# Token blocks of a gated linear attention and MoE layer: another order of the four engines' work, own buffers for the router's rows, a one-pass gate product

## The chip, the cores and the metric

One Trainium2 chip, one core. The metric is device time in microseconds (us) of one execution. A core has five engines with queues of their own: PE (TensorE, matmuls; PEld is its weight load), DVE (VectorE), ACT (ScalarE), POOL (GpSimd) and SP (SyncE, here the issuer of most DMAs). They meet only at semaphores. Everything is fp32; products that matter for precision are made of three f32r ("fp32r") products of a high and a low part.

## What is computed

```python
x = x + attn(layernorm(x))        # x: 2 x 8192 x 512, 16 heads of 32, chunks of 64
x = x + ffn(layernorm(x))
# attn
q, k, v = x@Wq+bq, x@Wk+bk, x@Wv+bv
alpha = 0.9 * sigmoid(silu(x@Wg1+bg1) @ Wg2 + bg2) + 0.1      # Wg1: 512 x 16
intra = softmax(causal(q k^T / sqrt(32))) v                   # within a chunk of 64
inter_t = q_t S ;  S = alpha_t * S + k_t v_t^T                # a state over all tokens
# ffn: 64 experts, top 8, 256 places each, hidden 384
routed = sum over the token's experts of w_e * down_e(silu(gate_e x) * up_e x)
shared = (silu(x @ gate) * (x @ up)) @ down
```

## The kernel before

`phase_tokens` goes over the 16384 tokens in 64 blocks of 256; `phase_experts` then goes over the 64 experts and is not touched. The change lies in `phase_tokens`.

For each block the kernel makes: the norm (`norm1`, `rstd1`, `shift1`, `normalise`), its transpose XT as high and low part (`xt`, `xt_evac`, `xt_low`), the gate (`gate1`: 512 to 16, `silu1`, `gate2`: 16 to 512, tanh and `alpha`), q, k, v (`project`, `values`), the running product of alpha within half chunks (`decays`), its inverse (`products`, `inverse`: two reciprocals on DVE), and with both the decayed q and k on POOL (`unpair`, `fold`, `decayed_k`, `decayed_q`). The inter part needs k turned back to tokens (`ktok`), four outer products (`state_updates`) and the state's steps (`state`). The attention proper has four units u = 0 to 3, each 128 tokens by 8 heads. A unit is a chain: `scores` (PE), `softmax_a` (mask, maximum, decayed scores; DVE), `exp` (eight exponentials with sums; ACT), `softmax_b` (divide; DVE), `turn_probs` (PE), `weights` (DVE), `outputs` (PE), `ot` (eviction; ACT). Then: `turn_out`, `residual` with the variance, `rstd2` (POOL), `norm2`, the transpose `x2t`, the router (`router`, `lt`, `turn_logits`, `route_a` to `route_c`, counts in `positions`), and the shared feed forward (`gate_up` 0 to 2, `gu`, `hidden`, `hidden_high`, `hidden_low`, `down`, `total`).

The order on each engine is written out by hand, one list per engine, in a loop over pairs of blocks (PE's body: 16 blocks). PE's step (L1057) is `feed(t)`, all of the feed forward of block t, and then `attend(t+1)`, all four units of block t+1 mixed with the projections of block t+2. The last `attend` projects a block 64 that doesn't exist. An engine stops at a wait, and all that is behind it in its queue stops too.

What ties the lists together beside the data are the buffers. PE writes every product other than scores, probabilities and outputs into four PSUM banks; `BANK_OF` says which job has which bank, and `take` (L709) waits until the bank's last job has been read. The router's transposed rows go into XT, the same buffer as those of the attention, so `x2t` on ACT (L603) waits until block t+1's values are made, and `xt_evac` (L545) until `gate_up` is done. KD, QD, PV, RI and AL exist once. POOL's order in the loop is `unpair`, `fold`, `decayed_k`, `rstd2(0)`, `decayed_q`, `rstd2(1)`, `rstd1` (L525 to L531). `gate2` (L756) is an f32 product; L762 is its matmul. The helper L729 to L731 (`split_product`) records all three-part products.

## Time and profile before

| | us |
|---|---|
| median of 3 runs (lowest, highest) | 4608.77 (4606.5, 4610.91) |
| the profiled execution's own time | 4610.58 |
| its span on the core | 4608.7 |
| granted TensorE clock, mean over the span | 0.992 |
| PE busy | 4433.4 (96%) |
| DVE busy | 3520.7 (76%) |
| ACT busy | 2271.6 (49%) |
| POOL busy | 1333.8 (29%) |

The span runs from the first instruction to the last. Busy time is the time in which at least one of an engine's instructions runs; a busy PE is not PE at its peak, because matmuls are pipelined and overlap in the record. So the length of a piece of PE's work is read here as its pitch, from its start to the start of the next piece. The token phase runs to about 3680, the expert phase from there to the end.

### The profile page before, as it was taken

Reading aid. Unit: us, or ns where it says so; the run is one execution under the profiler, and the core shown is the slowest. Engines: PE = TensorE matmul, PEld = TensorE weight load, DVE = VectorE, ACT = ScalarE, POOL = GpSimd, SP = SyncE. Lnnn points to the kernel's source line nnn. Section 1 sums busy time; section 2 is a strip of 40 time slices with the busy share of each in tenths; the row PEclk is TensorE's granted clock in tenths of the full one; section 3 lists DMA queues with packets and bytes.
Section 4 is the critical chain, followed back from the end, with each engine's and each line's share of the span. In section 5 each row is a group of like instructions: output and inputs, shape, how many; then the busy total and the mean of one; then the engine's idle time right before and its main releaser. Section 6 shows DMA issues by size and latency. Waiting matters only on the chain. (4 is left out here: it accounts for less than half of the span.)

```text
span 4608.7 us, 182901 instructions
## 1 busy us (share of the span) xinstructions
PE 4433.4 (96%) x74416; PEld 3859.5 (84%) x74416; DVE 3520.7 (76%) x7639; ACT 2271.6 (49%) x7475; POOL 1333.8 (29%) x1275
## 2 busy tenths in 40 slices
PE   6999999999999999999999999999999969999998
PEld 5888888888888888888888888888888769999998
DVE  5777777777777777777777777777777778888887
ACT  4444444444444444444444444444444446666665
POOL 2111111111111111222221111111111156666666
PEclk9999999999999999999999999999999989999999
DMA  2001001011010001000001000001010079999997
GB/s 67 32 31 31 31 31 36 32 35 33 31 31 32 32 31 32 32 31 31 32 32 35 31 31 32 31 31 36 32 36 32 32 242 266 270 265 270 267 267 194
DMA packets 195037, 358.24 MB, mean 78 GB/s; under 512 B 16736, under 2 KB 92896, under 8 KB 194352
## 3 DMA queue, kind: packets, MB, share of 16 engines
q1 hardware_dynamic: 160848, 269.47, 17.6%
q0 software_dynamic: 33632, 79.73, 7.8%
q8 instruction: 547, 8.96, 0.8%
q14 instruction: 10, 0.08, 0.0%
HBM read 243.87 MB, written 107.50 MB: 76 GB/s over the span
## 5 line engine op out<-in xcount | busy, mean ns | idle before, releaser
L591 ACT ACTIVATE PR<-PR,MX 128x64 f32<-128x64 f32 x2048 | 682.7, 335 | 736.6 <-DVE MX L1186 736.6
L477 POOL TENSOR_TENSOR RI<-PV,AL 128x512 f32<-128x512 f32 x65 | 78.7, 1212 | 2448.5 <-DVE PV L1140 2448.5
L729 PE MATMUL bank<-XTh,wsguh 128*128 128x256 f32 x1536 | 447.1, 291 | 0.1
L1678 PE MATMUL ebank<-XH,WH 128*128 128x256 f32 x1536 | 431.3, 281 | 7.3 <-DVE XL L1760 7.3
L730 PE MATMUL bank<-XTl,wsguh 128*128 128x256 f32 x1536 | 430.4, 280 | 0.0
L731 PE MATMUL bank<-XTh,wsgul 128*128 128x256 f32 x1536 | 430.4, 280 | 0.0
L1678 PE MATMUL ebank<-XH,WL 128*128 128x256 f32 x1536 | 429.8, 280 | 0.0
L1678 PE MATMUL ebank<-XL,WH 128*128 128x256 f32 x1536 | 429.6, 280 | 0.0
L1753 DVE TENSOR_TENSOR WL<-WS,WH 128x768 fp32r<-128x768 f32 (+1 forms) x455 | 370.8, 840 | 16.2
L591 ACT ACTIVATION_READ_ACCUMULATOR PR<-PR,MX 128x1 f32 x2048 | 383.0, 187 | 0.0
L1615 ACT ACTIVATE WH<-WS 128x768 fp32r<-128x768 f32 (+1 forms) x455 | 325.2, 747 | 26.6 <-DMA WS<-in_L_ffn_w_down_dram 26.6
L729 PE MATMUL bank<-XTh,wkh 128*128 128x256 f32 x1040 | 315.4, 303 | 0.0
L729 PE MATMUL bank<-XTh,wqh 128*128 128x256 f32 x1040 | 305.1, 293 | 0.0
L1678 PEld LDWEIGHTS ebank<-XH,WH 128*128 128x128 f32 x1536 | 289.4, 188 | 10.1 <-issue 7.7
L730 PE MATMUL bank<-XTl,wqh 128*128 128x256 f32 x1040 | 292.6, 281 | 0.0
L731 PE MATMUL bank<-XTh,wql 128*128 128x256 f32 x1040 | 292.5, 281 | 0.0
L730 PE MATMUL bank<-XTl,wkh 128*128 128x256 f32 x1040 | 291.4, 280 | 0.0
L731 PE MATMUL bank<-XTh,wkl 128*128 128x256 f32 x1040 | 291.2, 280 | 0.0
L1678 PEld LDWEIGHTS ebank<-XL,WH 128*128 128x128 f32 x1536 | 288.3, 188 | 2.5
L729 PEld LDWEIGHTS bank<-XTh,wsguh 128*128 128x128 f32 x1536 | 289.6, 189 | 0.6 <-issue 0.6
L730 PEld LDWEIGHTS bank<-XTl,wsguh 128*128 128x128 f32 x1536 | 290.0, 189 | 0.0
L1678 PEld LDWEIGHTS ebank<-XH,WL 128*128 128x128 f32 x1536 | 289.8, 189 | 0.0
(228 smaller groups left out, 13243.6 us busy)
## 6 DMA issues: line engine op xcount, KB each, us to landing
WS<-in_L_ffn_w_gate_dram SPq DMA_DIRECT2D x65, 768.0 KB
WS<-in_L_ffn_w_up_dram SPq DMA_DIRECT2D x65, 768.0 KB
WS<-in_L_ffn_w_down_dram SPq DMA_DIRECT2D x65, 768.0 KB
norm_rows<-XR SPq DMA_DIRECT2D x64, 576.0 KB, 3.5
X<-in_L_attn_x_dram SPq DMA_DIRECT2D x66, 512.0 KB, 3.7
out_dram<-X SPq DMA_DIRECT2D x64, 512.0 KB, 2.9
CR<-token_counts,count_at POOLq DMA_INDIRECT x136
XG<-norm_rows,row_at POOLq DMA_INDIRECT x132, 6.2
```

What stands on the lines that cost most here:

```text
L477: nc.gpsimd.tensor_tensor(inverse[:, :, 0:half], PV[:, :, :], running[:, :, HC:half:-1], ALU.mult).then_inc(folded.sem, 1)
L591: ins = nc.scalar.activation(PR[b][:, j, :], PR[b][:, j, :], ACT.Exp, bias=MX[b][:, j:j + 1], scale=1.0, accum_out=SU[b][:, j:j + 1])
L729: nc.tensor.matmul(out, sh, mh, start=first, stop=False)
L730: nc.tensor.matmul(out, sh, ml, start=False, stop=False)
L731: return nc.tensor.matmul(out, sl, mh, start=False, stop=last)
L1615: nc.scalar.activation(WH[t.buf][:, cols], WS[t.buf][:, cols], ACT.Copy).then_inc(wh_ready.sem, 1)
L1678: last = nc.tensor.matmul(bank[HID[m]][:, a * CAP:(a + 1) * CAP], w, x[odd][:, c, :], start=(c == 0 and i == 0), stop=(c == KC - 1 and i = ...
L1753: v.tensor_tensor(WL[t.buf][:, cols], WS[t.buf][:, cols], WH[t.buf][:, cols].bitcast(f32), ALU.subtract).then_inc(wl_ready.sem, 1)
```

## The change

In words:

- The router's transposed rows get buffers of their own, XB; `x2t` now waits for the last block's `gate_up` only, and `xt_evac` for the last projections. KD is now RI and s1 is t1, in place.
- `gate2` is one f32r product. `s1` and Wg2 lie in partitions 0, 32 and 64 as high, low and high part (`COPIES`), so that one product of 128 rows sums all three terms. `s1_high` (ACT) and `s1_low` (DVE, 32 partitions) are new; Wg1, Wg2 and bg1 are loaded three times in the setup, and Wg2 is split there.
- Unit 0 of block n = t+1 is moved into block t's feed part on all engines; `ktok` and the first half of `state` too. Units 1 to 3 stay beside the projections of block m = t+2.
- ACT: `normalise(p)`, p = t+3, ahead of `gu(n, 0)` and of the exponentials of unit 0. DVE: both reciprocals behind `weights(n, 3)`; `softmax_a` is split in two, `residual` and `route_b` too; `route_c` (the counts) is ahead of `route_rows`. POOL: `rstd2(0)` first, `rstd1` last.
- PE's jobs have other banks, and a job's wait is worked out from `JOBS` (bank, block ahead).
- The first and the last steps are written out; block 64 and SP's two last loads of X are gone.

```diff
+JOBS = {
+    "GU0": (2, 0), "RLT": (1, 0), "KTok0": (3, 1), "GU1": (0, 0), "KTok1": (1, 1), "GU2": (3, 0), "DN0": (2, 0), "DK": (0, 1),
+    "DN1": (1, 0), "G1": (3, 2), "Qa": (1, 2), "G2a": (2, 2), "G2b": (3, 2), "Ka": (1, 2), "ATr0": (3, 1), "Qb": (0, 2),
+    "Kb": (2, 2), "V0": (1, 2), "ATr1": (3, 1), "X2Ta": (2, 1), "X2Tb": (3, 1), "V1": (0, 2), "RL": (1, 1)}
+ORDER = list(JOBS)
+
...
+        XB = [sb(f"XB{i}", [P, KC, TB], f32r) for i in "hl"]
...
-        KD = sb("KD", [P, KC, TB])
+        KD = RI
...
             def unpair(t):
 
                 pool.wait_ge(inverted.sem, t.value(inverted))
-                pool.wait_ge(kd_ready.sem, t.value(kd_ready, back=1))
+                pool.wait_ge(scored.sem, t.value(scored, back=1))
+                pool.wait_ge(ktok_filled.sem, t.value(ktok_filled, back=1))
                 apart(pool, pool_apart)
...
+            def step(t):
+                n = t.next()
+                m = t.next(2)
+                p = t.next(3)
+                rstd2(n, 0)
+                unpair(m)
+                rstd2(n, 1)
+                fold(m)
+                decayed_k(m)
+                decayed_q(m)
+                rstd1(p)
 
             rstd1(Turn(0, 0))
...
+            def xt_evac(t, k):
+
+                act.wait_ge(v_filled.sem, t.value(v_filled, back=1))
+                act.wait_ge(q_filled.sem, t.value(q_filled, back=1))
+                act.wait_ge(k_filled.sem, t.value(k_filled, back=1))
+                act.wait_ge(xt_filled.sem, t.value(xt_filled, k))
+                nc.scalar.activation(XT[0][:, 2 * k:2 * k + 2, :], XT_BANK[k].rearrange("p (a b) -> p a b", a=2),
+                                     ACT.Copy).then_inc(xh_ready.sem, 1)
 
             def gate1(t):
                 act.wait_ge(g1_filled.sem, t.value(g1_filled))
                 act.wait_ge(s1_ready.sem, t.value(s1_ready, back=1))
                 nc.scalar.activation(t1[:, :], bank_of("G1")[0:GP, 0:TB], ACT.Tanh, bias=b1h[:, :], scale=0.5).then_inc(g1_tanh.sem, 1)
                 nc.scalar.activation(z1[:, :], bank_of("G1")[0:GP, 0:TB], ACT.Identity, bias=b1[:, :], scale=1.0).then_inc(g1_tanh.sem, 1)
+
+            def s1_high(t):
+                act.wait_ge(s1_made.sem, t.value(s1_made))
+                act.wait_ge(g2_filled.sem, t.value(g2_filled, back=1))
+                nc.scalar.activation(sg[:, :], s1[:, :], ACT.Copy).then_inc(s1h_ready.sem, 1)
...
+            def x2t(t, k):
+                act.wait_ge(gu_filled.sem, t.value(gu_filled, back=1))
+                act.wait_ge(x2t_filled.sem, t.value(x2t_filled, k))
+                nc.scalar.activation(XB[0][:, 2 * k:2 * k + 2, :], bank_of("X2Ta" if k == 0 else "X2Tb")[:, :]
+                                     .rearrange("p (a b) -> p a b", a=2), ACT.Copy).then_inc(x2h_ready.sem, 1)
...
+            def step(t):
+                n = t.next()
+                m = t.next(2)
+                p = t.next(3)
+                gate1(m)
+                exp(n, 1)
+                s1_high(m)
+                ot(n, 0)
+                q_evac(m, 0)
+                gate2(m, 0)
+                gate2(m, 1)
+                alpha(m)
+                exp(n, 2)
+                ot(n, 1)
+                k_evac(m, 0)
+                exp(n, 3)
+                ot(n, 2)
+                q_evac(m, 1)
+                k_evac(m, 1)
+                ot(n, 3)
+                x2t(n, 0)
+                x2t(n, 1)
+                lt(n)
+                normalise(p)
+                gu(n, 0)
+                hidden_high(n, 0)
+                exp(m, 0)
+                ktok_evac(m, 0)
+                gu(n, 1)
+                hidden_high(n, 1)
+                ktok_evac(m, 1)
+                router_exp(n)
+                gu(n, 2)
+                xt_evac(p, 0)
+                xt_evac(p, 1)
+                hidden_high(n, 2)
...
+            def take(job, t):
+
+                for name, at in jobs_back(job):
+                    if t.next(at).exists:
+                        ev, k = READ[name]
+                        pe.wait_ge(ev.sem, t.next(at).value(ev, k))
+                        break
                 return bank_of(job)
...
+                if k == 0:
+                    pe.wait_ge(a_masked.sem, t.next(-1).value(a_masked, 0))
...
+            def s1_low(t):
+                dve.wait_ge(s1h_ready.sem, t.value(s1h_ready))
+                v.tensor_tensor(sg[32:64, :], s1[32:64, :], sg[32:64, :].bitcast(f32), ALU.subtract).then_inc(s1_ready.sem, 1)
...
+            def step(t):
+                n = t.next()
+                m = t.next(2)
+                p = t.next(3)
+                scores_part(n, 1)
+                decay_part(n, 1)
+                silu1(m)
+                state(n, (2, 3))
+                s1_low(m)
+                softmax_b(n, 1)
+                weights(n, 1)
+                scores_part(n, 2)
+                decay_part(n, 2)
+                decays(m)
+                softmax_b(n, 2)
+                products(m)
+                weights(n, 2)
+                scores_part(n, 3)
+                decay_part(n, 3)
+                residual(n, 0)
+                variance2(n, 0)
+                softmax_b(n, 3)
+                weights(n, 3)
+                inverse(m, 0)
+                inverse(m, 1)
+                norm2(n, 0)
+                residual(n, 1)
+                variance2(n, 1)
+                values(m, 0)
+                norm2(n, 1)
+                x2t_low(n, 0)
+                x2t_low(n, 1)
+                values(m, 1)
+                norm1(p)
+                shift1(p)
+                hidden(n, 0)
+                scores_part(m, 0)
+                decay_part(m, 0)
+                hidden_low(n, 0)
+                route_a(n)
+                hidden(n, 1)
+                hidden_low(n, 1)
+                softmax_b(m, 0)
+                route_b(n)
+                hidden(n, 2)
+                xt_low(p, 0)
+                xt_low(p, 1)
+                hidden_low(n, 2)
+                weights(m, 0)
+                route_c(n)
+                route_rows(n)
+                state(m, (0, 1))
+                total(n, 0)
+                total(n, 1)
...
```

PE's step in full, in its order: gate_up(t, 0), scores(n, 0), turn_logits(t), ktok(n, 0), gate_up(t, 1), ktok(n, 1), xt(m) x2, gate_up(t, 2), down(t, 0), state_updates(n, 0), down(t, 1), state_updates(n, 1), turn_probs(n, 0), positions(t), the rest of down, scores(n, 1), gate1(m), outputs(n, 0), q(m) first half, gate2(m) x2, turn_probs(n, 1), scores(n, 2), k(m) first quarter, outputs(n, 1), k(m) second quarter, scores(n, 3), turn_out(n, 0), turn_probs(n, 2), q(m) third quarter, outputs(n, 2), q(m) last and k(m) third quarter, turn_probs(n, 3), k(m) last quarter, outputs(n, 3), half of values(m, 0), turn_out(n, 1), its other half, x2t(n, 0), half of values(m, 1), x2t(n, 1), its other half, the router's high and low part of n. The lists of DVE and ACT run half a step behind PE's: their step(t) begins with unit 1 of block n and ends with block n's feed forward and unit 0 of block m.

## Rows read from the trace of the kernel before

**Rows 1.** stages: us, then PE, PEld, DVE, ACT, POOL busy, granted clock, DMA

```profile
2000.00:2500.00 500.00, 490.44 (x9418) 417.87 (x9417) 376.99 (x844) 228.90 (x872) 100.45 (x90) 1.00 0.10 33
...
3700.00:3800.00 100.00, 75.73 (x513) 70.46 (x514) 80.49 (x141) 50.82 (x94) 55.97 (x57) 0.84 0.78 232
```

**Rows 2.** PE's timeline, scores(t, 0) of blocks: start us, us, line, out<-in, shape, count

```profile
73.49 0.67 PE L830 MATMUL sa<-QD,KD 32*32 32x64 f32 x32 [0.78 <-issue]
...
1934.07 0.44 PE L830 MATMUL sa<-QD,KD 32*32 32x64 f32 x32
...
1990.05 0.44 PE L830 MATMUL sa<-QD,KD 32*32 32x64 f32 x32
...
3621.73 0.43 PE L830 MATMUL sa<-QD,KD 32*32 32x64 f32 x27
```

**Rows 3.** PE's timeline, pieces of one block; [idle before, what ended it]

```profile
1997.98 1.97 PE L762 MATMUL bank<-s,wg 128*128 128x256 f32 x8 [0.30 <-DVE s L1122]
1999.78 0.60 PE L866 MATMUL pt_bank<-ident,PR 128*128 128x128 f32 x4
...
2000.34 0.28 PE L730 MATMUL bank<-XTl,wkh 128*128 128x256 f32 x1
2000.46 0.28 PE L731 MATMUL bank<-XTh,wkl 128*128 128x256 f32 x1
...
2019.32 0.66 PE L866 MATMUL pt_bank<-ident,PR 128*128 128x128 f32 x4 [0.17 <-DVE PR L1197]
```

**Rows 4.** DVE's costliest group, 2000 to 2500: busy us, mean ns | idle

```profile
L1140 DVE RECIPROCAL PV<-PV 128x256 f32<-128x256 f32 x18 | 31.4, 1744 | 0.0
```

**Rows 5.** POOL's timeline in the first block, where nothing holds it up

```profile
58.91 1.22 POOL L477 TENSOR_TENSOR RI<-PV,AL 128x512 f32<-128x512 f32 x1 [22.81 <-DVE PV L1140]
...
63.49 2.35 POOL L514 TENSOR_TENSOR KD<-KT,RI 128x1024 f32<-128x1024 f32 x1
65.79 2.17 POOL L504 TENSOR_TENSOR QD<-QT,AL 128x1024 f32<-128x1024 f32 x1
68.07 0.69 POOL L453 TENSOR_TENSOR rs<-ve,neg_half 128x2 f32<-128x2 f32 x1
```

**Rows 6.** DVE's timeline in the middle, three stretches of two blocks

```profile
1996.38 0.20 DVE L1196 RECIPROCAL RU<-SU 128x8 f32<-128x8 f32 x1 [0.67 <-ACT PR L591]
...
2020.01 0.69 DVE L1207 TENSOR_TENSOR WT<-pt_bank,AM 128x512 f32<-128x512 f32 x1 [0.75 <-PE pt_bank L866]
2022.29 0.55 DVE L1227 TENSOR_SCALAR XR<-X,mv,rs 128x512 f32<-128x512 f32 x1 [1.58 <-POOL rs L457]
...
2030.98 0.17 DVE L1106 TENSOR_SCALAR ve<-mv 128x2 f32<-128x2 f32 x1
2031.96 0.16 DVE L1112 SCALAR_TENSOR_TENSOR sh<-mv,rs 128x2 f32<-128x2 f32 x1 [0.81 <-POOL rs L453]
```

**Rows 7.** ACT's timeline: norm, exponentials of one unit, an eviction of KTok, a tanh

```profile
1978.40 1.51 ACT L541 ACTIVATE XN<-X,sh,rs 128x512 f32<-128x512 f32 x2
...
1993.58 0.35 ACT L591 ACTIVATE PR<-PR,MX 128x64 f32<-128x64 f32 x1 [5.78 <-DVE MX L1186]
...
1996.25 0.45 ACT L556 ACTIVATE t<-bank,b1h 128x256 f32<-128x256 f32 x1
...
2028.40 0.61 ACT L584 ACTIVATE KTok<-bank 128x512 f32<-128x512 f32 x1
...
2033.26 0.38 ACT L631 ACTIVATE TG<-bank 128x256 f32<-128x256 f32 x1 [2.33 <-PE bank L731]
```

**Rows 8.** SP's queue in the setup, one load

```profile
25.83 0.42 SPq L373 DMA_DIRECT2D bvb<-in_L_attn_bv_dram  x1
```

**Rows 9.** DVE's timeline, the last sums of the token phase

```profile
3677.62 1.39 DVE L1302 TENSOR_TENSOR X<-bank,X 128x512 f32<-128x512 f32 x2 [0.55 <-PE bank L731]
```

**Rows 10.** PE's timeline, first products of the expert phase

```profile
3721.23 0.42 PE L1678 MATMUL ebank<-XL,WH 128*128 128x256 f32 x1
3721.45 0.41 PE L1678 MATMUL ebank<-XH,WL 128*128 128x256 f32 x1
```

More of the change, by code:

```diff
@@ L33 @@
 GH = 16
+COPIES = (0, 32, 64)
 GP = 128
@@ new lines, in _ @@
+            router_exp(Turn(0, 0))
+            gu(Turn(0, 0), 2)
+            xt_evac(Turn(0, 2), 0)
+            xt_evac(Turn(0, 2), 1)
+            hidden_high(Turn(0, 0), 2)
+            with act.Fori(0, 30) as pair:
+                for odd in range(2):
+                    step(Turn(pair, odd))
+            for odd in range(60, 61):
+                step(Turn(0, odd))
+            gate1(Turn(0, 63))
+            exp(Turn(0, 62), 1)
+            s1_high(Turn(0, 63))
+            ot(Turn(0, 62), 0)
@@ L1049, in feed @@
                 down(t, 0, (0, 1))
[L1050 removed]
+                state_updates(n, 0)
                 down(t, 1, (0, 1))
[L1052 removed]
+                state_updates(n, 1)
+                turn_probs(n, 0)
+                positions(t)
                 down(t, 0, (2,))
                 down(t, 1, (2,))
[L1055 to L1064 removed]
+                scores(n, 1)
@@ new lines, in _ @@
+            decay_part(Turn(0, 0), 2)
+            decays(Turn(0, 1))
+            softmax_b(Turn(0, 0), 2)
+            products(Turn(0, 1))
+            weights(Turn(0, 0), 2)
+            scores_part(Turn(0, 0), 3)
+            decay_part(Turn(0, 0), 3)
+            residual(Turn(0, 0), 0)
+            variance2(Turn(0, 0), 0)
+            softmax_b(Turn(0, 0), 3)
+            weights(Turn(0, 0), 3)
+            inverse(Turn(0, 1), 0)
+            inverse(Turn(0, 1), 1)
+            norm2(Turn(0, 0), 0)
@@ new lines, in _ @@
+            residual(Turn(0, 0), 1)
+            variance2(Turn(0, 0), 1)
+            values(Turn(0, 1), 0)
+            norm2(Turn(0, 0), 1)
+            x2t_low(Turn(0, 0), 0)
+            x2t_low(Turn(0, 0), 1)
+            values(Turn(0, 1), 1)
+            norm1(Turn(0, 2))
+            shift1(Turn(0, 2))
+            hidden(Turn(0, 0), 0)
+            scores_part(Turn(0, 1), 0)
+            decay_part(Turn(0, 1), 0)
+            hidden_low(Turn(0, 0), 0)
+            route_a(Turn(0, 0))
@@ new lines, in _ @@
+            hidden(Turn(0, 0), 1)
+            hidden_low(Turn(0, 0), 1)
+            softmax_b(Turn(0, 1), 0)
+            route_b(Turn(0, 0))
+            hidden(Turn(0, 0), 2)
+            xt_low(Turn(0, 2), 0)
+            xt_low(Turn(0, 2), 1)
+            hidden_low(Turn(0, 0), 2)
+            weights(Turn(0, 1), 0)
+            route_c(Turn(0, 0))
+            route_rows(Turn(0, 0))
+            state(Turn(0, 1), (0, 1))
+            total(Turn(0, 0), 0)
+            total(Turn(0, 0), 1)
@@ new lines, in _ @@
+                    links[0], links[1] = 0, Turn(pair, odd)
+                    step(Turn(pair, odd))
+                    assert links[0] == LINKS, links[0]
+            for odd in range(60, 61):
+                links[0], links[1] = 0, Turn(0, odd)
+                step(Turn(0, odd))
+            links[0], links[1] = START + 61 * LINKS, None
+            scores_part(Turn(0, 62), 1)
+            decay_part(Turn(0, 62), 1)
+            silu1(Turn(0, 63))
+            state(Turn(0, 62), (2, 3))
@@ new lines, in _ @@
+            hidden_low(Turn(0, 62), 0)
+            route_a(Turn(0, 62))
+            hidden(Turn(0, 62), 1)
+            hidden_low(Turn(0, 62), 1)
+            softmax_b(Turn(0, 63), 0)
+            route_b(Turn(0, 62))
+            hidden(Turn(0, 62), 2)
+            hidden_low(Turn(0, 62), 2)
+            weights(Turn(0, 63), 0)
+            route_c(Turn(0, 62))
+            route_rows(Turn(0, 62))
+            state(Turn(0, 63), (0, 1))
+            total(Turn(0, 62), 0)
+            total(Turn(0, 62), 1)
@@ new lines, in _ @@
+            softmax_b(Turn(0, 63), 3)
+            weights(Turn(0, 63), 3)
+            norm2(Turn(0, 63), 0)
+            residual(Turn(0, 63), 1)
+            variance2(Turn(0, 63), 1)
+            norm2(Turn(0, 63), 1)
+            x2t_low(Turn(0, 63), 0)
+            x2t_low(Turn(0, 63), 1)
+            hidden(Turn(0, 63), 0)
+            hidden_low(Turn(0, 63), 0)
+            route_a(Turn(0, 63))
+            hidden(Turn(0, 63), 1)
+            hidden_low(Turn(0, 63), 1)
+            route_b(Turn(0, 63))
```

679 lines of the change are left out of this document (394 added, 285 removed).

## The prediction

> **What bounds the kernel now.** First the busy time by stretch: in the middle of the token phase PE is busy 490.4 of 500 us at a granted clock of 1.00, DVE 377.0, ACT 228.9, POOL 100.5 [rows 1]. PE bounds it. Then PE's timeline, for the length of a block: the first product of `scores(t, 0)` starts at 1934.07 and at 1990.05, a block of 55.98 us; over all 63 blocks from 73.49 to 3621.73 it is 56.32 [rows 2]. The 0.34 between the two are odd stalls of PE itself, some of them called "issue". Then I took the pitch (start to next start) of each piece of PE's order: a product of 256 columns 0.12, the unit of scores 1.36, of outputs 1.29, a set of four transposes 0.35, the two halves of the gate product together 1.80 [rows 3]. Summed with the least pitch each piece shows anywhere, a block is 53.1 us; the other 2.9 are short waits of PE: on V for the second and third chunk (0.35 each), on the second tile of the normalised rows (0.5), on the split of the router's rows (1.0), on `s1` (0.3), and small ones. So PE has at most 2.9 us of waits to lose per block, and the expert phase (after 3700) is untouched.
>
> **What PE's work becomes.** The gate product goes from f32, seen as eight instructions in 1.80 us, to four f32r ones, 4 x 0.12 = 0.48 [rows 3]: minus 1.3. The rest is the same matmuls in another order. PE's floor becomes 53.1 - 1.3 = 51.8 us per block. If nothing waited, 62 blocks would give 62 x 4.5 = 280 us. Whether that comes is a question of what each wait now ends on, since much is moved on the other three queues.
>
> **The new order, walked once round.** Names are those of the new `step(t)` of DVE, ACT and POOL: n, m, p are blocks t+1, t+2, t+3; PE's order runs half a step ahead, so its next `gate_up` is block n's. I start behind `weights(n, 3)` on DVE and follow what each engine must wait for, with the durations of the block shown.
>
> 1. POOL. DVE now does both reciprocals, 1.74 us each [rows 4], behind `weights(n, 3)`; before, they ran while the exponentials of units 2 and 3 were made, some 9 us earlier in the attention part. POOL's products start when they end. In the first block, where POOL runs without a gap, the first product of `unpair` starts at 58.91 and `rstd1` ends at 68.76 [rows 5]: 9.85 us for `unpair`, `fold`, `decayed_k`, `decayed_q`, `rstd1`. Two `rstd2` at the start are in it now (one exposed, 0.6), and `decayed_q` beside a busy DVE took 0.3 more than in that row. So `rstd1(p)` ends 3.5 + 10.75 + 0.3 (hops) = 14.5 us after `weights(n, 3)`.
> 2. DVE meanwhile: reciprocals 3.4, then norm2, residual, variance, values, norm2, the split, values and norm1, the same set that now runs from 2022.29 to 2031.15, 8.9 us with its own waits [rows 6]. It arrives at `shift1(p)` after 12.1 and waits **2.5 us**. Before, this wait was 0.8 (2030.98 to 2031.96 [rows 6]), because POOL had long been free. Everything of the feed part stands behind it on DVE.
> 3. PE passes x2t, values, the router and `gate_up(n, 0)` (2.9) and wants `scores(m, 0)` 0.8 us before `decayed_q` ends: a wait of 0.8.
> 4. ACT has `normalise(p)` before `gu(n, 0)`: 1.42 to its next start plus 0.38 for the tanh [rows 7], so `hidden(n, 0)` waits **1.95**. Before, hidden(0) came ahead of the norm.
> 5. DVE: hidden(0), scores_part, decay_part, hidden_low, route_a. ACT: `exp(m, 0)` 2.67 (1993.58 to 1996.25), ktok_evac 0.6, tanh 0.4 [rows 7]. hidden(1) stands behind all of these, 3.7 us from the reduction, while DVE has 1.5 us of work: waits **2.2**.
> 6. PE there: `ktok(m, 1)` has bank 1 after the turned logits, so it waits for route_a, 1.8; `gate_up(n, 2)` has bank 3 after KTok0, whose eviction is behind the exponentials, 0.6.
> 7. DVE at hidden_low **0.5**; at `weights` for the turned probabilities (0.69 from PE's start in 2019.32 to DVE's in 2020.01 [rows 3, 6]) 0.6, 0.8, 0.4 and 0.8, **2.6** in all.
> 8. Attention unit 1 of the next step, with blocks m and p: `s1_high(p)` is behind `exp(m, 1)` on ACT, `s1_low` on DVE waits for it: 2.67 + 0.42 against 2.4 us of DVE work, **0.75**. PE's gate product waits 1.9 there, its longest new stall. `s1_low` itself adds 0.4 of DVE.
> 9. The third unit's scores **0.7**, softmax_b of unit 3 **0.4**, and in the set of step 2 **1.5** (already in its 8.9).
>
> This closes a ring in which DVE hardly meets slack. Its length: DVE's work 377.0/500 x 56.3 = 42.4, s1_low 0.4, gaps between dependent small instructions 0.7, and the waits 2.5 + 1.95 + 2.2 + 0.5 + 2.6 + 0.75 + 0.7 + 0.4 + 1.5 = 13.1: **56.7 us**. PE has 51.8 of work in it and stalls 5 us. I take 56.8, for the back edge of DVE's loop, which now lies on the ring (before, DVE idled 1.1 or 0.6 there). Against 56.32 that is +0.5 per block: what the gate product saves goes into new waits.
>
> **The ends.** The setup has five more loads, 0.42 us each on SP's queue (25.83 is one such issue [rows 8]), ACT's and DVE's split of wg2 1.0: +3. DVE then starts the scores of unit 1 of block 0 at 79.3 (rstd1 ends at 68.8; scores 0, exponentials, two evictions of KTok, the split of block 1, state), 62 blocks of 56.8 follow, the last overlapped one is 53.4 (no norm1, no split, no wait for POOL), and block 63 alone takes 47.4: three units bare at 5.5 to 6.5 each, the norm, the router, then gate, up and down 17. End of the sums: 3 + 79.3 + 3521.6 + 53.4 + 47.4 = 3704.7, against 3677.62 + 1.39 = 3679.0 [rows 9]: +26. Block 64's projections, 25 us of PE, thus give little: they lay where block 63's attention waits anyway. SP loads two blocks less at the end and stores counts after the rows as before: nothing, it waits for DVE. `route_c` ahead of `route_rows` moves 1.1 us of DVE and changes no sum. The buffers XB free x2t from waiting for block m's V, and this wait was not the last to end before.
>
> The profiled execution took 4610.6 (span 4608.7), 1.8 above the median of the three runs; so 4610.6 + 26 - 2 = **4635 us**. A measurement of this kernel can tell about 0.2% (9 us) from no change.
>
> **Bounds of what the trace doesn't show.** Each of some 17 waits is a difference of hops that I read to 0.05: +-0.85 per block, +-53 us in all. `s1_low` on 32 partitions: between 0 and 0.43 (the full 256-column DVE row); I took 0.42. The DVE back edge: 0 to 1 us per pair, up to +30. Cold PE in the bare last block: 0 to 5.
>
> **Rivals.**
> - *The ring is shorter* (26%). If POOL is done sooner, because less of DVE's work runs beside it (63.49 and 65.79 show 2.35 and 2.17 [rows 5]), and the hops are at their short end, the ring is 55.4: 4635 - 62 x 1.4 = 4548. For it: the waits of PE that went, and block 0's POOL rows. It needs 56.4 to be even with before. Beyond it, the waits could dissolve nearly wholly (5%): PE's floor with 1 us of waits, 52.8: 4387. Against: the POOL chain alone puts 2.5 us on DVE, and the place of `exp` before the second `gu` stands in ACT's order.
> - *The ring is longer* (18%): the wait at the second `hidden` grows when gate_up(1) itself comes late, or the gate product's 1.9 us pushes unit 2: 58.0 per block, 4710. Decides as soon as DVE's lag at unit 1's scores_part is over 4 us behind PE.
> - *PE's clock falls in the waits* (4%). It was 0.84 in the stretch where PE was busy 76% and 1.00 at 98% [rows 1]; PE will be busy 91%. At the lower level a 256-column product took 0.21 against 0.12 [rows 10, 3]. If the 24 products behind the stall of step 6 run so, +2.2 per block, of which some 1.5 reach the ring: 4728. The Trainium skill, TensorE: Matmul & The Clock Gate, under the second failure mode (queue depth-cycling), says that frequent short idles between groups of matmuls can make the clock swing between its two levels. By that rule the time would be 4728; the trace so far has PE waits of 0.15 to 0.35 with 1.00 granted.
> - *It does little* (in the "same" below): the ring falls within 0.15 us of 56.4.
>
> **Chances and range.** My forecast case, 56.5 to 57.5 per block (4615 to 4680), has 37%, and the other cases 26, 5, 18 and 4; 10% lies within 0.2%. Faster by over 0.2%: 0.34 (26 + 5, and 3 of the borders); same 0.11; slower 0.55. The range takes in the short ring and the long one: 4535 to 4725. It leaves out the dissolved waits and the clock.
>
> **What would show it.** Right: PE busy near 91 to 92% in the middle with DVE near 76%; PE waits at the gate product on DVE's s1_low (1 to 2 us), at the second ktok on route_a, at unit 0's scores on QD; DVE's wait at `shift1` on POOL about 2.5 us instead of 0.8; the reciprocals directly ahead of POOL's products; a pitch of 56 to 57.5 between blocks. Wrong: a pitch under 56 with DVE's wait at `shift1` under 1.5, or PE at 97% busy: then the ring doesn't bind. A granted clock under 0.98 in the middle would be the third rival. The gate product should take 0.5 instead of 1.80 in every case.

## The result, and the profile after

4694.8 us median (4693.0 to 4695.4) against 4608.9 (4606.5 to 4610.9): ratio 1.0189, interval 1.0177 to 1.0202. The change makes the kernel **slower, by 86 us**. The forecast had the sign, and 4694.8 lies in its range, but it gave +26: the size was wrong by a factor of three.

Windows of the kernel after (columns as in [rows 1]): the middle, and the end of the token phase.

```profile
2000.00:2500.00 500.00, 469.02 (x9017) 401.62 (x9015) 378.18 (x832) 226.04 (x854) 100.54 (x90) 1.00 0.09 30
3700.00:3740.00 40.00, 28.77 (x737) 22.05 (x735) 23.59 (x59) 11.36 (x57) 0.54 (x1) 0.68 0.09 32
```

PE was busy 490.4 of 500 us before [rows 1], now 469.0, at the same full clock; no other engine took its place (DVE 76%, ACT 45%, POOL 20%). So nothing saturates. What sets the time is then a ring of hand-overs (one engine waits for the next, round to the first); the experiments below test that. DVE's timeline, from the end of a step's norm to the second tanh:

```profile
2077.11 1.75 DVE L1290 TENSOR_SCALAR ve<-mv 128x2 f32<-128x2 f32 x1
2079.68 0.16 DVE L1296 SCALAR_TENSOR_TENSOR sh<-mv,rs 128x2 f32<-128x2 f32 x1 [0.81 <-POOL rs L469]
2081.69 0.42 DVE L1485 SCALAR_TENSOR_TENSOR WG<-TG,bank 128x256 f32<-128x256 f32 x1 [1.85 <-ACT TG L673]
...
2087.46 0.42 DVE L1485 SCALAR_TENSOR_TENSOR WG<-TG,bank 128x256 f32<-128x256 f32 x1 [2.12 <-ACT TG L673]
```

POOL's timeline beside it, and what PE waits for in the same stretch:

```profile
2068.86 1.21 POOL L494 TENSOR_TENSOR RI<-PV,AL 128x512 f32<-128x512 f32 x1 [5.84 <-DVE PV L1328]
...
2071.25 0.54 POOL L473 TENSOR_TENSOR rs<-ve,neg_half 128x1 f32<-128x1 f32 x1
...
2074.27 2.41 POOL L529 TENSOR_TENSOR RI<-KT,RI 128x1024 f32<-128x1024 f32 x1
2076.64 2.20 POOL L521 TENSOR_TENSOR QD<-QT,AL 128x1024 f32<-128x1024 f32 x1
2078.95 0.70 POOL L469 TENSOR_TENSOR rs<-ve,neg_half 128x2 f32<-128x2 f32 x1
```

```profile
2078.99 0.44 PE L952 MATMUL sa<-QD,RI 32*32 32x64 f32 x32 [0.74 <-POOL QD L521]
2085.40 0.66 PE L912 MATMUL bank<-ident,RI 128*128 128x128 f32 x4 [1.13 <-DVE LG L1430]
2087.22 0.39 PE L853 MATMUL bank<-XBh,wsguh 128*128 128x256 f32 x1 [0.28 <-ACT KTok L627]
```

The waits that the forecast named are there, at nearly its sizes: `shift1` starts 2.40 us after the tiny `ve` would have been done at its usual 0.17 (forecast 2.5; before, 0.81 [rows 6]), the first and second `hidden` wait 1.85 and 2.12 (1.95, 2.2), PE's `scores(m, 0)` 0.74 (0.8). The sum over 500 us, from the view of waits (us, times, longest):

```profile
DVE WG L1485 <- ACT TG L673: 36.2, 18, 2.1
DVE WT L1400 <- PE pt_bank L989: 18.8, 26, 0.8
PE bank L912 <- DVE LG L1430: 10.2, 9, 1.2
DVE sh L1296 <- POOL rs L469: 7.3, 9, 0.8
```

The block: DVE's unit-1 scores (`L1372`) of block 0, block 62 and block 63, and the last sums:

```profile
83.80 0.69 DVE L1372 TENSOR_TENSOR PR<-sa,causal 128x512 f32<-128x512 f32 x1
...
3656.02 0.68 DVE L1372 TENSOR_TENSOR PR<-sa,causal 128x512 f32<-128x512 f32 x1
...
3711.79 0.68 DVE L1372 TENSOR_TENSOR PR<-sa,causal 128x512 f32<-128x512 f32 x1
...
3760.61 1.28 DVE L1497 TENSOR_TENSOR X<-bank,X 128x512 f32<-128x512 f32 x2
```

(3656.02 - 83.80)/62 = **57.62 us per block**, against 56.32 [rows 2] and the forecast's 56.8. The token phase ends at 3761.9 instead of 3679.0 [rows 9]: +82.9 of the spans' +84.2.

Most blocks take 57.2 to 57.5, some more. From the third block on, 15 overlapped ones are longer than 57.65 (from one `silu1` to the next), and 14 of these lose their time at one place, DVE's `weights(n, 2)`. Here are PE's and DVE's rows there in the block shown above (57.26, nearly the shortest) and in the longest (60.4), with a window of the longest:

```profile
2057.25 0.60 PE L989 MATMUL pt_bank<-ident,PR 128*128 128x128 f32 x4
2057.94 0.69 DVE L1400 TENSOR_TENSOR WT<-pt_bank,AM 128x512 f32<-128x512 f32 x1 [0.68 <-DVE FX L1324]
...
1013.98 0.38 PE L854 MATMUL bank<-XTl,wkh 128*128 128x256 f32 x1 [1.46 <-issue]
1022.40 0.69 DVE L1400 TENSOR_TENSOR WT<-pt_bank,AM 128x512 f32<-128x512 f32 x1 [3.88 <-issue]
...
1014.00:1018.00 4.00, 4.00 (x67) 3.49 (x71) 3.93 (x9) 2.55 (x16) 0.00 (x0) 0.57 0.02 4
```

From `turn_probs(n, 1)` to `turn_probs(n, 2)` PE has no wait in the block shown: DVE waits there for PE's own work (the FX that the record names was done at 2057.27). So the ring runs through PE in that stretch. In the long block PE stalls for 1.46 us in the K product ("issue"), its granted clock is 0.57 for the next 4 us, and DVE waits 3.88 instead of 0.68.

### The profile page after: what moved, and what is told of

It is laid out like the page before. It is cut to its first block and busy times, and to the rows that moved or that the text cites. A ratio compares the mean times of both kernels' runs of the same rounds, so it can differ in the third digit from the quotient of the medians.

```text
span 4692.9 us, 181989 instructions
## 1 busy us (share of the span) xinstructions
PE 4346.3 (93%) x73868; PEld 3795.6 (81%) x73868; DVE 3581.2 (76%) x7674; ACT 2286.5 (49%) x7515; POOL 1316.9 (28%) x1266
## 5 line engine op out<-in xcount | busy, mean ns | idle before, releaser
L473 POOL TENSOR_TENSOR rs<-ve,neg_half 128x1 f32<-128x1 f32 x128 | 69.2, 540 | 2589.6 <-DVE ve L1415 2589.3
L853 PE MATMUL bank<-XBh,wsguh 128*128 128x256 f32 x1536 | 442.8, 288 | 19.0 <-ACT KTok L627 18.5
L854 PE MATMUL bank<-XBl,wsguh 128*128 128x256 f32 x1536 | 430.4, 280 | 0.0
L855 PE MATMUL bank<-XBh,wsgul 128*128 128x256 f32 x1536 | 430.2, 280 | 0.0
L1400 DVE TENSOR_TENSOR WT<-pt_bank,AM 128x512 f32<-128x512 f32 x256 | 177.0, 692 | 200.6 <-PE pt_bank L989 142.2
L853 PEld LDWEIGHTS bank<-XBh,wsguh 128*128 128x128 f32 x1536 | 289.7, 189 | 34.6 <-ACT KTok L627 33.5
L854 PEld LDWEIGHTS bank<-XBl,wsguh 128*128 128x128 f32 x1536 | 289.8, 189 | 0.0
L855 PEld LDWEIGHTS bank<-XBh,wsgul 128*128 128x128 f32 x1536 | 289.5, 188 | 0.0
```

What stands on the lines that cost most here:

```text
L473: nc.gpsimd.tensor_tensor(rs2[:, k:k + 1], ve2[:, k:k + 1], neg_half[:, k:k + 1], ALU.pow).then_inc(rstd2_ready.sem, 1)
L853: nc.tensor.matmul(out, sh, mh, start=first, stop=False)
L854: nc.tensor.matmul(out, sh, ml, start=False, stop=False)
L855: return nc.tensor.matmul(out, sl, mh, start=False, stop=last)
L1400: v.tensor_tensor(WT[u % 2][:, :, :], pt_bank[:, :].rearrange("p (n k) -> p n k", k=P), AM[u % 2][:, :, :], ALU.add).then_inc(w_ready.sem, 1)
```

## Experiments

All run beside the kernel before, whose median was 4606.7 to 4607.6. "Pitch" is POOL's `rstd1` from block to block, as it mostly is (57.3 in the kernel after).

### One move at a time

**inv**: the reciprocals back ahead of the third unit.

```diff
                 products(m)
+                inverse(m, 0)
                 weights(n, 2)
                 scores_part(n, 3)
                 decay_part(n, 3)
+                inverse(m, 1)
                 residual(n, 0)
...
                 weights(n, 3)
-                inverse(m, 0)
-                inverse(m, 1)
```

> The changed kernel with both reciprocals back ahead of the third unit's work on DVE: inverse(m, 0) behind products(m), inverse(m, 1) behind decay_part(n, 3); all else as changed. Nothing is left out. Ring theory (a chain of hand-overs among DVE, ACT and POOL sets the block, 57.6 us in the changed kernel, and the wait for POOL at shift1 is a link of it): POOL starts its products some 9 us earlier, is done with rstd1(p) long before DVE asks, the wait at shift1/values (0.8 and 1.56 us of DVE) and PE's wait for QD ahead of scores(m, 0) go, and since the chain from there on is the same, 1.5 to 2.3 us per block are won: 95 to 140 us, 4555 to 4600. Rival A (the exponentials of units 2 and 3 come late behind the reciprocals, 3.5 us of DVE work ahead of weights(2) and (3), and the wait is only moved): the time stays at 4685 to 4700, with DVE's waits at the weights smaller and PE's idle moved to the scores of units 2 and 3. Rival B (what costs is PE's own stalls in unit 0, not POOL): within 10 us of 4694.

Measured: 4823.9, ratio 1.0463 [1.0446, 1.0481]. All three ideas miss: it is **129 us slower** than the kernel after, pitch 59.6. DVE's timeline in this run, `weights(n, 3)` to the second tile's residual:

```profile
2075.85 0.69 DVE L1400 TENSOR_TENSOR WT<-pt_bank,AM 128x512 f32<-128x512 f32 x1 [0.75 <-PE pt_bank L989]
2076.46 1.17 DVE L1422 TENSOR_SCALAR XR<-X,mv,rs 128x512 f32<-128x512 f32 x1
2080.60 0.69 DVE L1408 TENSOR_TENSOR X<-bank,X 128x512 f32<-128x512 f32 x1 [2.97 <-PE bank L1034]
```

From `weights(n, 3)` to `residual(n, 1)` PE, ACT and PE make and turn the last outputs: 4.75 us here and 4.76 in the kernel after. There the reciprocals (3.5 us) fill it, and `residual(n, 1)` waits 0.25. Moved away they leave it empty (2.97), and push `weights(n, 3)` 2.3 us back (13.7 us behind the start of `decays` instead of 11.4). And POOL gains nothing: its queue has `rstd2(n, 1)` between `unpair` and `fold`, which waits for that residual (5.29 us idle), so `fold` comes 2.3 later too.

**rstd**: `rstd1(p)` ahead of `decayed_q(m)`.

```diff
                 decayed_k(m)
-                decayed_q(m)
                 rstd1(p)
+                decayed_q(m)
```

> The changed kernel with POOL's rstd1(p) ahead of decayed_q(m) instead of behind it; nothing is left out. Ring theory: DVE's shift1 comes 1.75 us earlier, but QD comes later by rstd1's 0.4 us, and PE's scores(m, 0) wait for QD more: 0.4 to 0.9 us per block are won, 4640 to 4670. Rival (QD itself, through the scores, is what the ring goes through, and DVE's wait is slack): slower by 0.4 per block, 4715 to 4725.

Measured: 4772.5, ratio 1.035 [1.0332, 1.0367]: slower by 78 us, by more than the rival said. DVE's and POOL's timelines:

```profile
2054.89 0.17 DVE L1290 TENSOR_SCALAR ve<-mv 128x2 f32<-128x2 f32 x1
2055.88 2.10 DVE L1296 SCALAR_TENSOR_TENSOR sh<-mv,rs 128x2 f32<-128x2 f32 x1 [0.81 <-POOL rs L469]
```

```profile
2055.15 0.70 POOL L469 TENSOR_TENSOR rs<-ve,neg_half 128x2 f32<-128x2 f32 x1 [0.61 <-DVE ve L1290]
2055.81 2.16 POOL L521 TENSOR_TENSOR QD<-QT,AL 128x1024 f32<-128x1024 f32 x1
```

`ve` takes 0.17 now, but `shift1` itself takes 2.10 and ends with QD (2057.98 and 2057.97). Counted from the end of `decayed_k`, DVE leaves `shift1` after 3.44 us, against 3.16 in the kernel after: it gained nothing. And PE, whose wait for QD has grown to 2.02, runs slowly behind it, though not in every block (PE's timeline, then windows; 1530 is a block with as long a wait):

```profile
2058.11 0.44 PE L952 MATMUL sa<-QD,RI 32*32 32x64 f32 x32 [2.02 <-POOL QD L521]
2058.48 1.13 PE L966 MATMUL sa<-KT,QT 32*64 32x64 f32 x32
...
1530.24 0.44 PE L952 MATMUL sa<-QD,RI 32*32 32x64 f32 x32 [2.10 <-POOL QD L521]
1530.61 0.69 PE L966 MATMUL sa<-KT,QT 32*64 32x64 f32 x32
```

```profile
2050.00:2058.00 8.00, 6.04 (x43) 5.35 (x42) 5.82 (x10) 1.47 (x3) 7.36 (x5) 1.00 0.14 52
2058.00:2062.00 4.00, 3.89 (x105) 3.54 (x106) 2.01 (x4) 2.20 (x4) 0.00 (x0) 0.56 0.02 4
...
1530.24:1538.24 8.00, 7.59 (x146) 6.90 (x147) 4.02 (x10) 5.62 (x22) 0.00 (x0) 1.00 0.02 4
2058.11:2066.11 8.00, 8.00 (x127) 7.62 (x128) 3.55 (x8) 5.35 (x21) 0.00 (x0) 0.57 0.01 2
```

The granted clock is 0.56 there, near the lower level (1.2 of 2.4 GHz), and the second set of scores takes 1.13 instead of 0.69. The mean clock in the middle is 0.96. Over 60 blocks, by the clock in the 8 us behind the wait and the distance to the next block's scores: 21 blocks kept 1.00 and took 57.7 us (median), 21 had 0.79 and took 58.8, 18 had 0.57 and took 59.7. At full clock the move thus costs 0.4 per block, which is what the rival said, about 25 of the 78 us; the rest goes with the clock. This is the forecast's third rival, in a kernel that has one longer wait than the one forecast. The Trainium skill, TensorE: Matmul & The Clock Gate, under its second failure mode, says that frequent short idles between groups of matmuls can make the clock swing between its levels. This run agrees; in the kernel after the clock stays at 1.00 from 2000 to 2500, with waits up to 1.13, but fell to 0.57 behind the stall of 1.46 in the long block above.

**norm**: the norm behind the first tanh and its split.

```diff
-                normalise(p)
                 gu(n, 0)
                 hidden_high(n, 0)
+                normalise(p)
                 exp(m, 0)
```

> The changed kernel with ACT's normalise(p) behind gu(n, 0) and hidden_high(n, 0) instead of ahead of them; nothing is left out. Ring theory: the first tanh comes 1.4 us earlier, hidden(n, 0) waits 0.5 instead of 1.9 us, the exponentials follow when they did (ACT's work is the same) or 0.3 later, so hidden(n, 1) gives some of it back: between 0.5 and 1.4 us per block won, 4605 to 4665. Rival (the second hidden, behind normalise, the exponentials, the eviction and the tanh, is the link and the first hidden only slack before it): within 10 us of 4694.

Measured: 4602.3, ratio 0.9987 [0.9978, 0.9997], pitch 55.8: **-92 us**, 3 us beyond the best that the ring theory gave. DVE's timeline: the first `hidden` follows `shift1` with no wait, and the 1.85 us gained come through but for 0.4, which the second returns (2.52 instead of 2.12).

```profile
2084.87 0.16 DVE L1296 SCALAR_TENSOR_TENSOR sh<-mv,rs 128x2 f32<-128x2 f32 x1 [0.81 <-POOL rs L469]
2085.07 0.42 DVE L1485 SCALAR_TENSOR_TENSOR WG<-TG,bank 128x256 f32<-128x256 f32 x1
...
2091.24 0.42 DVE L1485 SCALAR_TENSOR_TENSOR WG<-TG,bank 128x256 f32<-128x256 f32 x1 [2.52 <-ACT TG L673]
```

**comb**: the three edits together.

> The three moves together: the reciprocals early on DVE, rstd1(p) ahead of decayed_q(m) on POOL, gu(n, 0) and hidden_high(n, 0) ahead of normalise(p) on ACT; nothing is left out. Ring theory: the links lie one behind the other, so the gains add up, less what the next wait takes: 2.5 to 3.5 us per block, 4480 to 4540, faster than both kernels. Rival (the same microseconds are counted twice, each move frees the same slack): no better than the best of the three alone, 4570 to 4600.

Measured: 4842.4, ratio 1.0509 [1.0491, 1.0526], blocks of 59.0 and 60.5 in turn. A miss, of the kind that inv and rstd make likely: 129 + 78 - 92 = +115 against the kernel after by adding, +148 measured. What the 33 more are wasn't looked for.

### The gate product

**gate** is the kernel after, **bgate** the kernel before, each with the other's gate product.

```diff
--- gate
-                s1_high(m)
...
-                s1_low(m)
...
-                    last = nc.tensor.matmul(b[:, a * TB:(a + 1) * TB], wg2[:, m * P:(m + 1) * P], sg[:, :], start=True, stop=True)
+                    last = nc.tensor.matmul(b[:, a * TB:(a + 1) * TB], wg2[:, m * P:(m + 1) * P], s1[:, :], start=True, stop=True)
--- bgate
                     q_evac(n, 0)
+                    s1_high(n)
...
                     silu1(n)
+                    s1_low(n)
```

> The changed kernel with the gate's second product back in f32 (eight instructions, about 1.8 us of PE instead of 0.87), without s1_high on ACT and s1_low on DVE and their waits; nothing of the result is left out. Theory A (the ring): in the changed kernel's timeline, with DVE's silu1 at 0, PE's gate product waits for s1_low until 3.07 and turn_probs starts at 3.94. With the old product PE can start it at 2.2, when the Q product ahead of it ends, and needs 1.8: turn_probs starts at about 4.0, the same. So 0 to +0.2 per block: 4690 to 4710, although PE works 0.9 to 1.3 us more per block. Theory B (PE's work bounds, as before the change): +0.9 to +1.3 per block, 4750 to 4775. Theory C (s1_low and the wait ahead of it, 1.25 us of DVE, stand on the ring in full): -1.2 per block, 4620.

> The kernel before with the gate's second product alone changed: split f32r product, s1_high on ACT behind q_evac(n, 0), s1_low on DVE directly behind silu1; order and all else as before. Theory A (PE bounds the kernel before, and its wait for s1 grows by the two added hops, q_evac 0.8 + s1_high 0.4 + s1_low 0.4 us, more than the 0.9 to 1.3 us of work saved): between -0.4 and +0.8 us per block, 4585 to 4660. Theory B (PE has other work while the split is made, the saving comes in full): -0.9 to -1.3 per block, 4525 to 4555.

Measured: gate 4666.1, ratio 1.0127 [1.0111, 1.0144]: **-29 us** although PE works more (477.7 of 500 us). That is none of its three ideas; it lies between A and C. bgate 4630.3, ratio 1.0051 [1.0034, 1.0068]: **+24 us** although PE works less (479.3 instead of 490.4). In both the cheap product is a loss. PE's timeline in gate: the old product starts as soon as the Q product ends, and the turned probabilities follow 3.74 us after `silu1`, 3.94 in the kernel after (whose rows are the last two here). That is 0.2 of the 0.46 per block; the rest isn't explained.

```profile
2033.40 1.89 PE L872 MATMUL bank<-t,wg 128*128 128x256 f32 x8
2035.13 0.60 PE L975 MATMUL pt_bank<-ident,PR 128*128 128x128 f32 x4
```

```profile
2048.07 0.71 PE L886 MATMUL bank<-sg,wg 128*128 128x256 f32 x4 [0.89 <-DVE sg L1310]
2048.94 0.66 PE L989 MATMUL pt_bank<-ident,PR 128*128 128x128 f32 x4 [0.15 <-DVE PR L1390]
```

In bgate, where theory A held, the view of waits of PE has, in 500 us, nearly what the product saves (11.1). It had 1.7 of such waits before, so they alone would leave the time about as it was; what makes it 24 us longer wasn't read.

```profile
PE bank L776 <- DVE sg L1140: 10.6, 9, 1.3
```

### Is it one chain? The same work at two places, and a link shortened

**padon** and **padoff**: one more VectorE instruction per block.

```diff
+            def pad():
+                v.bn_stats(st1[:, 0, :], bvb[:, :])
--- padon
                 hidden(n, 0)
+                pad()
                 scores_part(m, 0)
--- padoff
                 route_a(n)
+                pad()
                 hidden(n, 1)
```

> The changed kernel with one more VectorE instruction per block, a bn_stats over 128x512 into a tile that is dead at that point (0.69 us, 0.60 in a row of others), between hidden(n, 0) and scores_part(m, 0); the result is untouched. DVE is busy 378 of 500 us. Theory A (the chain through DVE, the exponentials and the next tanh sets the block, and this place is a link of it): it comes through in full, +0.6 to +0.7 per block, 4730 to 4740. Theory B (DVE is only 76% busy and such work hides): within 10 us of 4694.

> The changed kernel with the same extra VectorE instruction (bn_stats over 128x512, 0.6 to 0.69 us) put behind route_a(n), where DVE waits 2.1 us for the second tanh; the result is untouched. The run with it ahead of scores_part(m, 0) gave +37 us. Theory A (DVE has slack at this place, not at the other): within 6 us of 4694. Theory B (any work added to DVE counts): +37 again, 4731.

Measured: padon 4731.5, ratio 1.0271 [1.0254, 1.0288], **+37 us**, 0.59 per block, in full; padoff 4694.1, ratio 1.0194 [1.0178, 1.0209], **-0.7 us**. DVE's share of busy time says nothing about either.

**foldcut**: POOL's chain shortened by 0.8 us. It leaves out most of one scaling, so its attention values differ; the expert phase is as long as in the kernel after (930.9 us, 931.0).

```diff
-                first = halves(running[:, :, 0:HC])
-                nc.gpsimd.tensor_tensor(first, first, bc(r_mid[:, :], HC), ALU.mult).then_inc(folded.sem, 1)
+                first = halves(running[:, :, 0:1])
+                nc.gpsimd.tensor_tensor(first, first, bc(r_mid[:, :], 1), ALU.mult).then_inc(folded.sem, 1)
```

> The changed kernel with the last product of fold on POOL (the running products times r_mid, 128x512, 1.06 us) cut to one column of each segment (128x16, about 0.25 us), with all its semaphores: this part of the scaling is left out, so its attention values differ; every wait and every other instruction stays. Theory A (POOL's chain from the reciprocals to decayed_q is a link of the ring): QD, rstd1 and with them shift1 and PE's scores(m, 0) come 0.8 us earlier, and most of it comes through: -0.6 to -0.8 per block, 4645 to 4660. Theory B (the wait at shift1 only shows work that another engine's chain covers): within 10 us of 4694.

Measured: 4644.1, ratio 1.0078 [1.0062, 1.0094]: -51 us, 0.82 per block. The instruction went from 1.05 to 0.24 us (POOL's timeline of this run), so its 0.81 came through in full:

```profile
2048.96 0.24 POOL L510 TENSOR_TENSOR AL<-AL,r_mid 128x16 f32<-128x16 f32 x1
```

**body8**: twice as many loop back edges on PE.

```diff
-            with nc.Fori(0, 24, 8, engines=[pe.engine], hint_back_edge=True) as pair:
-                for odd in range(16):
+            with nc.Fori(0, 24, 4, engines=[pe.engine], hint_back_edge=True) as pair:
+                for odd in range(8):
```

> The changed kernel with PE's loop over bodies of 8 blocks, six passes, instead of 16 blocks, three passes; nothing is left out. In the changed kernel the blocks at PE's back edges took 60.5, 58.8 and 58.3 us against 57.3. Theory A (the ring has no slack for a stall of PE, each back edge adds 1 to 3 us): three more of them, +3 to +10 us, 4697 to 4705, and six long blocks in the row of pitches, every 8. Theory B (they are absorbed): the same time and no pattern of 8.

Measured: 4687.0, ratio 1.0172 [1.0158, 1.0187], 8 us faster; neither theory. Long blocks are now at five of the six places every 8, but of 58.6, 58.1, 57.8, 58.1 and 58.1 instead of 60.5, 58.8 and 58.3: more of them, each smaller. Those 8 us can't safely be put down to the shorter body: with bodies of 16 the blocks at the back edges differ as much from kernel to kernel (63.4, 56.6 and 58.0 in foldcut; 55.6, 55.5 and 56.0 in ng, whose other blocks take 55.5). What sets them is open.

### Towards the best order

**ng** is norm and gate together; **ngu** is norm with `gu(n, 1)` ahead of `ktok_evac(m, 0)`; **ngk** is ng with `ktok_evac(m, 0)` ahead of `exp(m, 0)`; **ngv** is ng with the instruction of `ve` in another form; **ngkv** is all but ngu.

```diff
--- ngu
                 exp(m, 0)
+                gu(n, 1)
                 ktok_evac(m, 0)
-                gu(n, 1)
--- ngk
+                ktok_evac(m, 0)
                 exp(m, 0)
-                ktok_evac(m, 0)
--- ngv
-                v.tensor_scalar(ve1[:, :], mv1[:, :, 1], EPS, None, ALU.add).then_inc(var1_ready.sem, 1)
+                v.tensor_tensor(ve1[:, :], mv1[:, :, 1], eps_t[:, :], ALU.add).then_inc(var1_ready.sem, 1)
```

> The changed kernel with gu(n, 0) and hidden_high(n, 0) ahead of normalise(p), as in the run before, and gu(n, 1) ahead of ktok_evac(m, 0) as well; nothing is left out. Theory A (the second hidden, waiting 2.5 us for its tanh behind the exponentials and the eviction, is now a link): the tanh comes 0.5 us earlier, PE's gate_up(n, 2) has its bank 0.4 later, which is inside the slack: -0.3 to -0.5 per block against the 4602 of that run, 4570 to 4585. Theory B (softmax_b(m, 0) behind the exponentials is the link, or PE's bank): 4595 to 4625.

> The changed kernel with two pieces undone: the gate's second product in f32 again without its split, and gu(n, 0) with hidden_high(n, 0) ahead of normalise(p) on ACT; nothing is left out. The two lie at different places of the chain (start of the step; middle). Theory A (one chain, the gains add): 4695 - 92 - 29 = 4574, range 4565 to 4585. Theory B (behind the first gain another path, PE at 96%, becomes the limit): 4590 to 4605.

> As the run before it, and ktok_evac(m, 0) ahead of exp(m, 0) on ACT. Theory A (with the norm moved, PE's gate_up(n, 2) waits 0.2 us for that eviction's bank, and its work from there to turn_probs sets DVE's next step): PE gains 0.2 us, the exponentials and the second hidden come 0.1 to 0.55 later, which has slack: -0.1 to -0.2 per block, 4562 to 4570. Theory B (the exponentials and the second tanh behind them are the link): +0.1 to +0.5 per block, 4580 to 4605.

> As the first of these runs, with DVE's variance + eps of norm1 (128x2) as a tensor_tensor with a tile of eps instead of a tensor_scalar. In the changed kernel that small instruction takes 1.75 us and ends with POOL's decayed_q, against 0.17 where POOL is idle. Theory A (this form of DVE's instruction is held up while POOL's product runs, a tensor_tensor isn't; POOL's rstd1 stands behind decayed_q anyway): it takes 0.2 us, rstd1 starts when it did, and the time stays within 6 us of the first run. Theory B (DVE waits for something of POOL that isn't the form of the instruction): it still takes 1.5 to 1.8 us. Theory C (the hold-up was on the chain): 30 us or more faster.

> The changed kernel with the gate product in f32, gu(n, 0) and hidden_high(n, 0) ahead of normalise(p), ktok_evac(m, 0) ahead of exp(m, 0), and variance + eps of norm1 as a tensor_tensor; nothing is left out. If both of the last two gains (10 and 12 us against 4576) are real and at different places of the chain they add: 4553 to 4558. If they are the same slack, 4562 to 4568.

| run | us | ratio to before | pitch |
|---|---|---|---|
| ngu | 4618.0 | 1.0023 [1.0013, 1.0033] | 56.1 |
| ng | 4575.7 | 0.9931 [0.9918, 0.9945] | 55.5 |
| ngk | 4565.9 | 0.9911 [0.9896, 0.9926] | 55.4 |
| ngv | 4564.0 | 0.9903 [0.9888, 0.9918] | 55.4 |
| ngkv | 4553.3 | 0.9884 [0.9869, 0.9900] | 55.2 |

ng: 4694.8 - 92.5 - 28.7 = 4573.6 by adding; 4575.7 measured. The gains add, as in one chain. ngu missed: the second `hidden` did come 0.46 earlier, but 16 us were lost against norm. PE's timelines of norm and of ngu show the link: `gate_up(n, 2)` needs the bank of KTok0, and from there PE's own work leads to `turn_probs(m, 0)`.

```profile
2090.99 0.38 PE L853 MATMUL bank<-XBh,wsguh 128*128 128x256 f32 x1 [0.21 <-ACT KTok L627]
```

```profile
2045.61 0.39 PE L853 MATMUL bank<-XBh,wsguh 128*128 128x256 f32 x1 [0.42 <-ACT KTok L627]
```

That gave ngk, with the eviction earlier instead of later: -10 us against ng. Such steps are small: all executions of ngk (4561.8 to 4568.6) and ngv (4561.4 to 4568.6) lie below those of ng (4572.2 to 4579.3), but the intervals of the ratios overlap or touch. ngkv **beats both kernels**, by 54 us (1.2%) and 141 us. ngv's 12 us are not explained: `ve` is still held up, as the view of its line over all blocks shows (ns: least, median, most):

```profile
L1278 DVE TENSOR_TENSOR ve<-mv,eps_t x64: 163/1745/1904, 34.5 to 3510.5; 128x2 f32<-128x2 f32 x64
```

## Why the prediction was right and wrong

**Right: the mechanism and the sign.** PE went from 98% to 94% busy (forecast 91 to 92%), and DVE, ACT and POOL, and PE in one stretch, hand each other a ring. padon, padoff, foldcut and norm are four direct readings of it: at the two places on the ring (padon, foldcut) 0.6 and 0.8 us counted in full, norm's 1.85 came through but for 0.4, and the same 0.6 us off it (padoff) counted nothing.

**Wrong: the length of the ring, step by step.** The failed step is the sum 42.4 + 0.4 + 0.7 + 13.1, taken as 56.8 us per block where 57.62 was measured (the rounded terms give 56.6, with DVE's work unrounded 56.65). The block shown after is 57.26, from one `silu1` to the next on DVE's timeline. Its waits stand so:

| wait | forecast | measured |
|---|---|---|
| `shift1` for POOL, the hold of `ve` in it (steps 1, 2) | 2.5 | 2.39 |
| `hidden(n, 0)`, `hidden(n, 1)` (4, 5) | 1.95, 2.2 | 1.85, 2.12 |
| `hidden_low` (7) | 0.5 | 0.48 |
| four `weights` (7) | 2.6 | 2.89 |
| `s1_low` (8) | 0.75 | 0.90 |
| scores, softmax_b (9) | 0.7, 0.4 | 0.77, 0.38 |
| the set of step 2 | 1.5 | 1.47 |
| sum | 13.1 | 13.25 |

So the waits were right. The rest was not: 57.26 - 13.25 = 44.0, against 43.5. Of this DVE's busy time without the hold of `ve` is 43.63 - 1.58 = 42.05 (forecast 42.4 + 0.4), and the term that was mis-sized is the 0.7 for gaps between dependent small instructions. The five such gaps that the timeline lists make 0.79; 34 shorter ones between its rows, which it doesn't list, make 1.16 more, and the forecast had put them at nothing. The window of that block:

```profile
2045.00:2102.26 57.26, 53.85 (x1058) 46.20 (x1057) 43.63 (x96) 26.35 (x102) 11.21 (x10) 1.00 0.09 32
```

That is 0.6 us per block in all, 37 us over 62 blocks. The other 0.36 between 57.26 and the mean of 57.62 are the long blocks (60.5, 58.8, 58.3 at PE's back edges and many of 57.7 to 58), for which the forecast had 0.15. It let the rest vanish in PE's new slack. PE does idle 6%, but not in the stretch up to `turn_probs(n, 2)`, and there a stall of PE goes straight to DVE. Together 0.8 x 62 = 50 us, nearly the whole error of 58 us in the profiled execution (4694.6 against 4637). The remainder is at the ends: the start 1.5 later than forecast, the last overlapped block 55.8 instead of 53.4, block 63 alone 50.1 instead of 47.4, where the clock was 0.68 ("Cold PE", 0 to 5 in the bounds), and 1.3 in the expert phase.

The forecast had bounded this at +-0.85 per block, and the error lies just inside. The value inside the bound was chosen as if all gaps too short to be listed and PE's odd stalls were free. Step 2 has a slip beside it: 3.4 + 8.9 are 12.3, not 12.1; measured from the first reciprocal to `ve` it is 12.0.

**Right, but only half of the cause: POOL's lateness.** Step 1 says that POOL's products start when the reciprocals end, and so they do: POOL's first product waits 5.84 us for them, and `rstd1` ends 14.6 after the first reciprocal begins (forecast 14.5). foldcut shows that the length of this chain counts. But the forecast took their new place for the reason of the loss, and inv shows that the old one is worse. The second tile's `rstd2(n, 1)` stands in POOL's queue between `unpair` and `fold`, and its variance is ready 0.1 us before POOL comes to it (2071.16 and 2071.25). So reciprocals that end earlier can't bring `fold` forward.

**Steps 3 and 6 on PE**: its wait for QD 0.74 (0.8), for route_a 1.13 (1.8), for KTok0 0.28 (0.6), for the gate's split 0.89 (1.9). All smaller: PE ran later than walked. In the kernel after none of these could be seen to matter, and after norm the one for KTok0 does, as ngu shows.

**The gate product.** The forecast had "minus 1.3" on PE, and 1.15 us of wait and work on DVE (0.75 + 0.4). From its start to the turned probabilities it takes 0.87 (2048.07 to 2048.94), not 0.48, so minus 0.9; DVE pays 1.31 (0.90 + 0.41). It is a net loss of 29 us inside the new order.

**So the 86 us are**: the norm ahead of the first tanh +92, the f32r gate product +29 (each by undoing it), and everything else together (the unit beside gate and up, own buffers, no block 64, counts at once) 4575.7 - 4607.0 = **-31**. (This adds up to 90: norm and gate together gave 2 less than apart, and the kernel before was 2 faster beside them.) Those four were not tried one by one. The change contains a gain; two of its moves bury it.

**Rivals.** The shorter ring (26%) did not come, since POOL was not sooner; norm and gate together reach its number by other means (55.5 per block and 4576; its text 55.4 and 4548). The clock (4%) stayed at a mean of 1.00 in the middle, with a drop in the longest block, and fell in rstd. The longer ring (18%, 58.0 per block, 4710) was nearer to 57.62 than the forecast case, but by luck: neither of its two causes is seen (the second `hidden` waits 2.12, PE at the gate product 0.89).

## What to carry to other kernels

When no engine is over 95% busy in the stretch, look for the chain, and test a link with one dummy instruction on either side of a wait: here it cost its full length times the number of blocks on the ring, and off it nothing. A long instruction should be put where the engine waits anyway (the reciprocals here), and a short one that feeds another engine ahead of a long one that feeds nobody soon (the tanh ahead of the norm). When a ring of many hand-overs is summed, take the gaps from busy time against the block's length and not from the listed waits, which leave out the short ones, and add the odd stalls of every engine on it: slack elsewhere in that engine's queue does not absorb them where another waits for what comes next.
